# First tile: who asks for x's second half, when T's mask and B are asked for, and a warm-up of short and long products

## The reference

```python
def lora_add(base, inp, A, B):          # 16 LoRAs of rank 16, one per batch entry
    t = einsum('bri,bni->bnr', A[idx], inp)
    return base + einsum('bor,bnr->bno', B[idx], t) * 0.5
gate = lora_add(x @ W_gate.T, x, A_gate, B_gate)
up   = lora_add(x @ W_up.T,   x, A_up,   B_up)
act  = silu(gate) * up
down = lora_add(act @ W_down.T, act, A_down, B_down)
m    = max(|down|, axis=-1)             # at least 1e-5
y    = (down / m) @ levels[w_2bit].T * (m * scale) + bias
out  = x + y
```

## Time and profile before

| | us |
|---|---|
| median of three runs (910.3 to 911.4) | 911.34 |
| the profiled execution's own time | 911.69 |
| its span | 909.8 |

### The profile page before, as it was taken

One profiled execution on the slowest core, in us unless ns is written; L12 is line 12 of the kernel. 1 busy time (PEld: TensorE's weight loads), 2 busy tenths in 40 slices (PEclk: granted clock), 3 DMA queues, 4 the chain that ended last, 5 costly groups with the idle time before them and its releaser, 6 DMA issues.

```text
span 909.8 us, 13814 instructions
## 1 busy us (share of the span) xinstructions
PE 891.7 (98%) x3998; PEld 721.7 (79%) x3998; DVE 349.3 (38%) x757; ACT 260.3 (29%) x450; POOL 82.4 (9%) x114
## 2 busy tenths in 40 slices
PE   6899999999999999999999999999999999999997
PEld 6688888888888887888888888888888888888885
DVE  3664345222632334422353224533254322552225
ACT  2533252111522224211252113421134111422112
POOL 1011003000030000300003100031000210110200
PEclk9899999999999999999999999999999999999999
DMA  4564111111112011120111102111011111201001
GB/s 128 140 185 141 46 53 33 45 35 30 42 44 56 23 33 50 32 63 16 44 47 40 51 12 56 44 40 41 15 53 55 35 35 30 60 24 32 26 14 47
DMA packets 44997, 45.38 MB, mean 50 GB/s; under 512 B 13168, under 2 KB 31472, under 8 KB 44944
## 3 DMA queue, kind: packets, MB, share of 16 engines
q1 hardware_dynamic: 42640, 41.72, 16.8%
q10 hardware_dynamic: 2176, 2.89, 1.1%
q0 software_dynamic: 128, 0.26, 0.1%
HBM read 36.44 MB, written 8.39 MB: 49 GB/s over the span
## 4 chain that ended last, share of the span: by engine, by line
PE 95%; DVE 1%; SPq 1%; issue 1%; DMA 1%; ACT 1%; DVEq 0%
PE pw_up L1766 26%; PE pw_gate L1766 24%; PE pw_down L1839 24%; PE ps_misc L1867 6%; PE pw_td L1828 5%; PE pw_down L1852 2%; PE pw_up L1808 2%; PE ps_misc L1766 2%; PE pw_gate L1808 2%; PE ps_misc L1859 1%; DMA low_room<-pair_masks 1%; SPq L317 0%; SPq L329 0%; ACT wt_split L1003 0%; DMA plan_room<-places 0%
## 5 line engine op out<-in xcount | busy, mean ns | idle before, releaser
L1839 PE MATMUL pw_down<-wd,wact_split 128*128 128x512 f32 x960 | 232.5, 391 | 0.0
L1766 PE MATMUL pw_up<-wxs,wgu 128*128 128x512 f32 x948 | 229.4, 391 | 0.0
L1839 PEld LDWEIGHTS pw_down<-wd,wact_split 128*128 128x128 f32 x960 | 180.2, 188 | 44.5
L1766 PE MATMUL pw_gate<-wxs,wgu 128*128 128x512 f32 x864 | 213.6, 396 | 0.5 <-DVE wgu L1152 0.5
L1766 PEld LDWEIGHTS pw_up<-wxs,wgu 128*128 128x128 f32 x948 | 178.4, 188 | 38.6
L1766 PEld LDWEIGHTS pw_gate<-wxs,wgu 128*128 128x128 f32 x864 | 161.7, 190 | 34.5 <-DVE wgu L1152 1.2
L1391 DVE TENSOR_TENSOR wact_full<-pw_up,wact_full 128x512 f32<-128x512 f32 (+1 forms) x87 | 60.1, 690 | 295.8 <-PE pw_up L1808 293.6
L1022 ACT ACTIVATE wact_full<-pw_gate 128x512 f32<-128x512 f32 (+1 forms) x80 | 47.7, 596 | 277.3 <-PE pw_gate L1808 277.3
L1034 ACT ACTIVATE wact_split<-wact_full 128x512 fp32r<-128x512 f32 x80 | 50.5, 631 | 69.5 <-DVE wact_full L1391 69.4
L1396 DVE TENSOR_TENSOR wact_split<-wact_full,wact_split 128x512 fp32r<-128x512 f32 x80 | 55.6, 695 | 26.6 <-ACT wact_split L1034 26.4
L817 POOL TENSOR_TENSOR rows<-rows,bias 128x512 f32<-128x512 f32 x28 | 35.8, 1288 | 220.8 <-DMA rows<-x_tok 219.6
(11 more groups left out here) (134 smaller groups left out, 673.0 us busy)
## 6 DMA issues: line engine op xcount, KB each, us to landing
out<-rows SPq DMA_DIRECT2D x121, 64.0 KB, 1.6
rows<-x_tok SPq DMA_DIRECT2D x112, 64.0 KB, 1.8
rows<-w_gu SPq DMA_DIRECT2D x8, 512.0 KB, 4.2
x_raw<-x_feat SPq DMA_DIRECT2D x60, 64.0 KB, 1.8
x_more<-x_feat SPq DMA_DIRECT2D x59, 64.0 KB, 1.7
wb_raw<-b_rows SPq DMA_DIRECT2D x32, 92.0 KB, 2.8
low_room<-b_rows SPq DMA_DIRECT2D x32, 80.0 KB, 2.5
rows<-w_down SPq DMA_DIRECT2D x9, 256.0 KB, 4.3
```

Source lines behind the costliest of these rows:

```text
L1766: last = nc.tensor.matmul(bank, w, wxs[:, xp, k, :], start=(n == 0 and k == 0), stop=False, skip_group_check=(f == 0))
L1839: last = nc.tensor.matmul(pw_down[:, s, :], wact(ap, f)[:, s * P:(s + 1) * P], wd[:, wp, f, :], start=(f == 1 and n == 0), stop=False)
```

## The change

- The eight second entries of x (`x_more`): GpSimd asks for five of them (3 to 7, was 6 and 7), ScalarE for three (0 to 2, the first ahead of the high part of x's first half, the others behind it; was 3 to 5), SyncE for none.
- SyncE's list in `wide_program` begins with T's mask, then the LoRA numbers and B.
- Chunk 2's weights are split ahead of B and T on ScalarE and VectorE; on ScalarE the split also stands ahead of the requests for W_down's chunks 0 and 1.
- In the first tile the second copy of T's high part (rows 64 to 95) is made by GpSimd, as a product with ones, instead of by ScalarE.
- `plan_listed` is raised twice: SyncE and ScalarE, which wait for one, begin after two of the four small copies of line 1560, and GpSimd waits for two.
- The early warm-up is 13 products of 256 columns and 17 of 512 (was 30 of 256); the later one 7 of 256 (was 14).

```diff
--- before.py
+++ after.py
@@ -58,15 +58,15 @@
 
 
 
-EARLY_WARM_UP = 30
-WARM_UP = 14
+EARLY_WARM_UP = 13
+LONG_WARM_UP = 17
+WARM_UP = 7
 
 LAST_BY_SP = [range(0, 4), range(0, 2), range(0, 1), range(0, 2)]
 LAST_BY_ACT = [range(0), range(2, 4), range(1, 4), range(2, 4)]
 
-FROM_ACT = 3
-
-FROM_POOL = 6
+
+FROM_POOL = 3
 PLAN_COLUMNS_STEP = 8
 WQ_FROM = FC - KC
 
@@ -623,11 +623,9 @@
                                  .rearrange("a t n -> (a t) n")).then_inc(done, 16)
 
             def wide_program():
-                for e in range(0, FROM_ACT):
-                    load_x_entry(sp, wide_place(0, ENTRIES + e), x_more[:, e, :], x_more_in)
+                load_mask(sp, 0, mask_gu, mask_gu_in)
                 idx = wide_loras(0)
                 load_wide_b(sp, idx, 0)
-                load_mask(sp, 0, mask_gu, mask_gu_in)
                 load_wide_ad(sp, idx, 0)
                 load_wgu(sp, 3)
                 load_wd(sp, 2)
@@ -820,6 +818,10 @@
             def wide_program():
                 for e in range(FROM_POOL, ENTRIES):
                     load_x_entry(pool, wide_place(0, ENTRIES + e), x_more[:, e, :], pool_x_in)
+                for g in range(2):
+                    pool.wait_ge(t_masked, g + 1)
+                    pool.tensor_tensor(wt_split[2 * PAIR:STACK, g, :], t_full[:, g, :],
+                                       ones[0:PAIR, :].to_broadcast([PAIR, WIDE]), ALU.mult).then_inc(t_hi_again, 1)
                 wide_split_bd(0, first=True)
                 wide_split_a(1)
                 pool.wait_ge(const_in, 48)
@@ -840,7 +842,7 @@
             pool.memset(ones[:, :], 1.0).then_inc(ones_ready, 1)
             pool.memset(plan_columns, 0.0).then_inc(plan_cleared, 1)
             pool.wait_ge(ones_ready, 1)
-            pool.wait_ge(plan_listed, 1)
+            pool.wait_ge(plan_listed, 2)
             for slot, e in enumerate((0, WENTRIES - 1)):
                 load_a(pool, lora_at(pool, wide_place(0, e)), first_a[:, slot, :], first_a_in)
             flag = pair_flag(pool)
@@ -997,9 +999,10 @@
                 nc.scalar.activation(wb_split[0:2 * PAIR, f % 2, :, 0:WIDTHS[f]], wb_raw_chunk(f), ACT.Copy
                                      ).then_inc(b_hi, 1)
 
-            def wide_t_hi(tile, g):
+            def wide_t_hi(tile, g, first):
                 act.wait_ge(t_masked, 2 * tile + g + 1)
-                for first_row, done in ((0, t_hi), (2 * PAIR, t_hi_again)):
+
+                for first_row, done in (((0, t_hi),) if first else ((0, t_hi), (2 * PAIR, t_hi_again))):
                     nc.scalar.activation(wt_split[first_row:first_row + PAIR, g, :], t_full[:, g, :], ACT.Copy
                                          ).then_inc(done, 1)
 
@@ -1053,27 +1056,28 @@
                     for k in range(KC):
                         nc.scalar.activation(wa_split_chunk(HI, k), wa_raw_chunk(first_a, k), ACT.Copy
                                              ).then_inc(a_hi, 1)
+                    load_x_entry(act, wide_place(0, ENTRIES), x_more[:, 0, :], x_more_in)
                 wide_x_hi(tile, 0, first)
                 if first:
-                    for e in range(FROM_ACT, FROM_POOL):
+                    for e in range(1, FROM_POOL):
                         load_x_entry(act, wide_place(0, ENTRIES + e), x_more[:, e, :], x_more_in)
                     load_wgu(act, 2)
                 wide_x_hi(tile, 1, first)
                 if first:
+                    split_hi_wgu(2)
                     load_wd(act, 0)
                     load_wd(act, 1)
                     wide_b_hi(tile, 0, first)
                     wide_b_hi(tile, 1, first)
-                    wide_t_hi(tile, 0)
-                    wide_t_hi(tile, 1)
-                    split_hi_wgu(2)
+                    wide_t_hi(tile, 0, first)
+                    wide_t_hi(tile, 1, first)
                     split_hi_wd(0)
                 else:
                     wide_act_hi(tile - 1, FC - 1, False)
                     wide_b_hi(tile, 0, first)
                     wide_b_hi(tile, 1, first)
-                    wide_t_hi(tile, 0)
-                    wide_t_hi(tile, 1)
+                    wide_t_hi(tile, 0, first)
+                    wide_t_hi(tile, 1, first)
                     wide_td_copy(tile - 1)
                     wide_td_hi(tile - 1)
                 for f in range(FC):
@@ -1434,13 +1438,13 @@
                 wide_x_lo(tile, 0)
                 wide_x_lo(tile, 1)
                 if first:
+                    split_lo_wgu(2)
                     wide_b_lo(tile, 0)
                     wide_b_lo(tile, 1)
                     wide_mask_t(tile, 0, pw_gate, first)
                     wide_mask_t(tile, 1, pw_up, first)
                     wide_t_lo(tile, 0)
                     wide_t_lo(tile, 1)
-                    split_lo_wgu(2)
                     split_lo_wd(0)
                 else:
                     wide_act_lo(tile - 1, FC - 1)
@@ -1560,7 +1564,8 @@
                         copied = nc.vector.tensor_copy(plan[row:row + 1, 0:BATCH // 2]
                                                        .rearrange("p (t e) -> p t e", t=TILES),
                                                        by_half[:, :, half, :])
-                copied.then_inc(plan_listed, 1)
+
+                    copied.then_inc(plan_listed, 1)
                 then(nc.vector.tensor_copy(sorted_idx, ps_plan[32:33, :]))
 
                 then(tt(tile_rows[64:65, :], ps_plan[64:65, 0:BATCH:WENTRIES],
@@ -1942,6 +1947,9 @@
             for _ in range(EARLY_WARM_UP):
                 nc.tensor.matmul(pw_td[:, 0:TILE], wgu_chunk(HI, 1)[:, 0, 0, :], wgu_chunk(HI, 1)[:, 0, :, :],
                                  start=True, stop=True)
+            for _ in range(LONG_WARM_UP):
+                nc.tensor.matmul(pw_td[:, :], wgu_chunk(HI, 1)[:, 0, 0, :], wgu_chunk(HI, 1)[:, 0:2, :, :],
+                                 start=True, stop=True)
             flag = pair_flag(pe)
             with pe.If(flag == 0):
                 general_program()
```

## The result

| | before | changed |
|---|---|---|
| median at first measurement (us) | 911.37, four runs, 910.3 to 911.92 | 905.13, four runs, 904.69 to 907.95 |
| profiled execution's own time and span | 911.69, 909.8 | 907.95, 906.1 |

The ratio is 0.9939, with a 95% interval of 0.9917 to 0.9962: 6.2 us faster at the median, where 6.8 were forecast. One of the 51 executions of the kernel before that ran beside the experiments took 1115.98 us, at a mean clock of 0.754, and is left out throughout.

A forecast was written before the change was run, and what follows sets the result against it. TensorE, busy 98% of the span, bounds the kernel; only gaps and slow stretches can give. Terms: T 3.4, LoRA products 0.9, chunk 2's weights 0.5, clock 2.4, less 0.3: 6.8 us, median 904.5 (903.7 to 905.3); full range 902.4 to 907.3.

The forecast's parts named there:

- The branch stays where it is: TensorE's start: the branch begins at 11.0 us, takes 3.95 and ends at 14.95, as before.
- it waits for the queue to drain: Rival: the branch follows the last early product by 1.55 us, ends at 16.6 to 17.0; total 905.7; chance 0.12.
- The warm-up ends in time: Longer early warm-up ends at 15.4 at most, costing 0 to 0.3 us; chunk 0 starts at 16.0.
- the bound: Latest end of the early warm-up if the clock rises where it did: 15.4 us.
- x's second half by 20 us: GpSimd's five requests, 1.13 us apart, land x's second half at 19.1 to 20.0 us; the 1.2 us gap goes.
- The slow rival: GpSimd can't keep five transfers in the air: x's second half ready at 28.1, total near 915; chance 0.04.
- Chunk 2's weights are hidden: Weights land at about 21.4, are split between 21.5 and 24.0, hidden as long as B lands later.
- T's copies: GpSimd's two copies (1.04 us each) and VectorE's two low parts (0.68 each) run in a row, 25.65 to 29.1.
- Without it: Rival without contention on T's copies: T's products at 28.0 instead of 29.1, total 903.1 to 903.5; chance 0.22.
- A gap of 1.1 us: TensorE's wait for T, from 28.0 to 29.1, behind which the products were not to slow down.
- the gap for silu: Ahead of chunk 3: TensorE there at 39.6, silu of chunk 2 done at 39.9, a new gap of 0.3 us.
- T's 3.4: Gain from T's products coming at 29.1 instead of 32.50: 3.4 us of the total 6.8.

The follow-up runs named there:

- old warm-up: Changed kernel with the warm-up of before, 30 short early products and 14 late ones: 905.91 us, ratio 0.9948.
- old requests: Changed kernel with x's second half asked for as before (SyncE three, ScalarE three, GpSimd two): 910.46 us, ratio 0.9997.
- new order: Changed kernel, T's four copies on ScalarE, first ones first, chunk 2's high part behind B's, low part behind T's: 906.75 us, ratio 0.9955.
- copies on ScalarE: Changed kernel with T's second high copies back on ScalarE, none on GpSimd: 905.77 us, ratio 0.9943.
- products in the gap: Eight 512-column products made for nothing while TensorE waits for T: on the changed kernel 907.27 us (0.9957), on the kernel before 910.96 us (0.9995).
- before with products in the gap: Kernel before with eight 512-column products made for nothing ahead of the wait for T, nothing else: 910.96 us, ratio 0.9995.

## Why the prediction was right

The forecast was 904.5 for the median and 904.9 for the profiled execution; measured were 905.13 (905.41 over all 15 executions) and 907.95. So the median came out as forecast and the profiled execution did not, and three of the prediction's own signs failed in the profiles. The granted clock was to be 1.00 from 29 to 40 us: it fell in all three profiles of the changed kernel. The prediction was to be wrong if the gap ahead of T's products was over 2.5 us: it was 2.3, 2.5 (2.52) and 3.0. The wait for T was to be released by GpSimd: VectorE's low part released it.

The path that the prediction drew is seen in the profile of the old warm-up, the one with the change's order in which the weights landed early. First mask, T's products, chunk 2 and chunk 3 start there at 25.12, 28.98, 30.23 and 39.92; the forecast was 24.9, 29.1, 30.0 and 39.9. The median execution, 905.13, puts chunk 3 at 39.9 (less 865.2) and, with the clock held, T's products at 29.0. That is an estimate, as no profile shows such an execution of the changed kernel. That the errors of 0.1 to 0.4 us below cancel to nothing, and that the clock held in more than half of the executions, is luck. By its steps:

- *The branch stays where it is.* Right: 11.3 + 3.66 = 14.96, while TensorE's last early product ended 1.25 us later than before. The rival that it waits for the queue to drain falls: in the second profile of the changed kernel the branch ended at 14.6 (10.8 + 3.84) and the early products ran until 15.35.
- *The warm-up ends in time.* Right, at 14.66 in the first profile: its 17 long products took 4.04 us, the full rate (12 in 2.88), so the clock had risen before them. In the second they took 5.21 us and ended at the bound. Chunk 0 started at 15.98 to 16.03, forecast 16.0. That this is worth anything was not shown.
- *x's second half by 20 us.* Right: landed at 19.95, forecast 19.1 to 20.0, GpSimd's spacing 1.13 us as in its two requests before, landings 2.9 us. The slow rival falls. The run with the old requests shows that this move carries the gain, and its profile that it does so by taking x off SyncE's list ahead of B. T itself waited for x's second half in one profile alone, that of the new order.
- *Chunk 2's weights are hidden.* This step failed. They were to land at 21.4, by the 4.1 us of before; the landing took 5.9, 6.3 and 6.5 us in the three profiles of the changed kernel, and VectorE's list then runs without a break: weights 1.23, B's two low parts 0.68, first mask. In six of the eight profiles with this order the first mask starts 3.06 or 3.07 us after the weights' split begins (in the other two it waits for B). So it came at 26.10 instead of 24.9. The weights' share of that is 0.4 us: B landed at 24.52, against 23.7 to 24.2, and at 1.15 us behind it the first mask would have come at 25.67 without them. The prediction had named the price of the weights, up to 1.2 us, and not taken it.
- *T's copies.* Four operations in a row were to take 3.44 us from 25.65; that is 3.5 from the first mask's end. Measured from the first mask's start: 3.86 against a forecast of 4.2. Contention is real (2.41 us for two operations of 0.68), and the price was 0.3 us too high. Without it the prediction has 28.0 in one place and a total lower by 1.4 us in two others; 28.0 is 1.1 us lower than 29.1. The run with the copies on ScalarE had T's products 3.43 us behind the first mask.
- The two errors leave T's products at 29.96 in this execution, 0.9 us late, and 0.1 us early, at 28.98, where the weights landed early.
- *The clock.* "A gap of 1.1 us" became 2.3, and behind it the clock fell in the profiled executions. The prediction said what that would mean, but took it from a gap of 2.5 us on. With the clock held, 10.94 us lie between T's products and chunk 3 against a forecast of 10.5 plus 0.3 us of gap. The four LoRA products take 1.25 us of that, not 0.9, and the gap for silu did not open. The fall costs 1.3 to 2.6 us more.
- *The terms do not stand alone.* The sum gave 2.4 us to the clock. In the kernel before, products in the gap gave 0.8 us in the profile and nothing in the times, since chunk 3's feed lay only 1.4 us ahead of TensorE. The term was right only in company with T's 3.4.

The Trainium skill ("TensorE: Matmul & The Clock Gate", Part 1, What you observe) puts the moment of the rise within 500 ns either way from run to run, and the prediction gave it no weight. The profiles differ by more, and they decide: the 17 long products took 4.04, 5.21 and 4.13 us in the three of the changed kernel. The 1.17 us more of the second are 2.3 us at the low clock, an estimate, so the clock rose at about 12.5 us there and before 10.6 in the first. What cost time was not the rise but the later fall: five of 15 executions of one program are 2 to 4 us slower, and the three of them that were profiled all have it.

## What to carry to other kernels

In a fixed order of transfers and splits, ask of each step that is moved ahead when its data lands beside the new traffic, not how long the step takes: a 1.2 us operation that waits for a 5.9 us landing holds everything queued behind it. Of a gap, ask what releases the step behind it: x's requests were worth moving for the sake of B, which stood behind them in SyncE's list. A wait in an issuing engine's list also spaces out the requests behind it; taking it away can cost more than it gives, as it did where W_down was asked for ahead of B's landing. And an idle stretch just ahead of a dense one is worth shortening for the clock's sake only where the next feed is early enough to use it.

## What the runs showed of the hardware

- A subtraction with two SBUF operands on VectorE and a copy from SBUF on GpSimd took turns: two of each, alone 0.68 and about 1.04 us, began before the other engine's had ended but ended one behind the other, 0.55, 0.90 and 0.55 us apart, the last 3.0 us after the first began.
- The taken branch to `wide_program` stopped TensorE's sequencer for 3.5 to 4.5 us in the fourteen profiles, and the products already handed over ran on beneath it; what fills that time and ends with it is free.
- The 512 KB of chunk 2's weights took 4.1, 4.2 and 4.5 us to land in the three profiles with x's second half asked for as before, and 4.3 to 6.8 us in the eleven in which GpSimd asks for five of its entries.
- The clock's fall to 1.2 GHz came with gaps ahead of T's products of 1.4 to 3.1 us in nine profiles and did not come with gaps of 0.6 to 2.5 us in four, nor in one without a gap there. Nor did it come behind gaps ahead of x's second half of 1.2, 1.3, 1.5 and 2.4 us (before, before with products in the gap, new order, old requests). The length of the gap did not separate them. The fall is not tied to the gap's end either: it came 0.5 us before T's products (29.7) in the second profile of the changed kernel and 1.9 us behind them (33.0) with products in the gap. It came later where the early warm-up had run slower, so where the clock had first risen later: at 30.9 to 31.1 where the 17 long products took 4.0 to 4.2 us, at 32.1 with 4.65, at 32.8 to 33.0 with 5.0 and 5.1, but at 29.7 and 30.4 in two with 5.2 and 5.4. That the place of the gap decides, counted from the rise, is a rival to its length that no run here tests.
